# Last row's router scratch moved out of `wout`, longer runs for the final reads, a quarter of the final adds on GpSimd

## The reference, cut to what matters

```python
idx, wts = _router(x, gate_w, e_bias)                 # 6 of 64 experts for each token
shared = _relu2(x @ shared_up_w.T) @ shared_down_w.T
routed = _moe(x, idx, wts, w1, w2)                    # each expert takes at most 64 tokens
return shared + routed

h = _relu2(einsum('ecd,eid->eci', xd, w1))            # in _moe: xd are the tokens in each expert's slots
yd = einsum('eci,edi->ecd', h, w2)
y_assign = yd[e_flat, slot] * gate
zeros((T, D)).at[tok].add(y_assign)
```

## Time and profile before

| | |
|---|---|
| median of 3 runs | 1371.82 us (1371.63 to 1372.96) |
| the profiled execution | 1371.9 us, of which the span from first to last instruction is 1370.1 us |
| busy: PE, DVE, ACT, POOL | 1145.9 us (84%), 912.0 us (67%), 658.6 us (48%), 567.1 us (41%) |
| DMA | 159.56 MB, 116 GB/s over the span |
| chain that ended last | PE 55%, DVE 19%, POOL 7%, issue 7%, ACT 6%, DMA 4% |

### The profile page before, as it was taken

How to read it: one execution, slowest core, us unless ns; L and a number is a source line. 1 busy time by engine, 2 the same in 40 slices (tenths; PEclk the granted TensorE clock), 3 DMA queues, 4 the chain that set the end, 5 groups by cost and what they waited for, 6 DMA issues and landing times.

```text
span 1370.1 us, 24377 instructions
## 1 busy us (share of the span) xinstructions
PE 1145.9 (84%) x8378; PEld 741.5 (54%) x8380; DVE 912.0 (67%) x1850; ACT 658.6 (48%) x1575; POOL 567.1 (41%) x725
## 2 busy tenths in 40 slices
PE   2799998898899888988999988989999978877940
PEld 2355556665555557655555566655555566644520
DVE  4487785565788875656888875656887755671427
ACT  3655423666455524656445335666555235630630
POOL 1255561220377760210577831200777712133760
PEclk9999999999999998998999998999999999989975
DMA  7366442300243314101343332001333625058888
GB/s 312 118 206 196 156 156 74 94 2 20 87 145 108 107 43 118 48 2 35 120 129 101 116 80 70 25 21 39 129 123 106 195 76 162 10 196 268 155 198 313
DMA packets 120137, 159.56 MB, mean 116 GB/s; under 512 B 11632, under 2 KB 82928, under 8 KB 119280
## 3 DMA queue, kind: packets, MB, share of 16 engines
q1 hardware_dynamic: 106384, 131.73, 31.0%
q0 software_dynamic: 9216, 19.98, 5.7%
q10 hardware_dynamic: 4416, 6.29, 1.3%
HBM read 104.55 MB, written 40.83 MB: 106 GB/s over the span
## 4 chain that ended last, share of the span: by engine, by line
PE 55%; DVE 19%; POOL 7%; issue 7%; ACT 6%; DMA 4%; SPq 0%; POOLq 0%; DVEq 0%; ACTq 0%
PE bank L1187 12%; PE bank L1229 5%; DVE pool_c L1689 5%; PE bank L1110 5%; PE bank L1410 3%; PE bank L1367 3%; PE bank L1395 2%; PE bank L1332 2%; PE bank L1223 2%; PE bank L1216 2%; PE bank L1208 2%; PE bank L1300 2%; POOL joint L2198 2%; PE bank L1497 2%; POOL xn L2205 2%
## 5 line engine op out<-in xcount | busy, mean ns | idle before, releaser
L1187 PE MATMUL bank<-xm,joint 128*128 128x512 f32 x544 | 272.8, 626 | 20.2 <-DVE pool_c L1689 15.6
L2198 POOL TENSOR_TENSOR joint<-joint 128x512 f32<-128x512 f32 x128 | 168.5, 1318 | 225.3 <-DVE joint L1705 221.2
L1689 DVE SCALAR_TENSOR_TENSOR pool_c<-bank,params,pool_c 128x511 f32<-128x511 f32 (+2 forms) x216 | 161.1, 747 | 84.8 <-ACT pool_c L812 79.4
L1187 PEld LDWEIGHTS bank<-xm,joint 128*128 128x128 f32 x544 | 99.9, 197 | 123.9 <-issue 93.3
L1889 DVE TENSOR_REDUCE nmax<-bank 128x1 f32<-128x384 f32 (+3 forms) x176 | 109.6, 637 | 60.6 <-PE bank L1368 59.8
L1229 PE MATMUL bank<-wout,pool_c 128*128 128x256 f32 x512 | 125.1, 388 | 3.4 <-DVE pool_c L1730 3.4
L851 ACT ACTIVATE joint<-bank,dt_ 128x64 f32<-128x64 f32 x512 | 112.0, 342 | 28.7 <-PE bank L1110 28.7
L1229 PEld LDWEIGHTS bank<-wout,pool_c 128*128 128x128 f32 x512 | 98.6, 196 | 38.7 <-issue 23.3
L821 ACT ACTIVATE pool_c<-pool_c 128x512 f32<-128x512 f32 x64 | 40.2, 629 | 143.5 <-DVE pool_c L1689 143.5
L2192 POOL DMA_INDIRECT xslot<-xrow,slots x96 | 97.3, 1013 | 26.6 <-issue 21.9
L1730 DVE TENSOR_TENSOR pool_c<-xn,pool_c 128x512 f32<-128x512 f32 x64 | 90.0, 1405 | 19.1 <-POOL xn L2205 19.0
(11 more groups left out here) (272 smaller groups left out, 2379.1 us busy)
## 6 DMA issues: line engine op xcount, KB each, us to landing
pool_b<-dA_rows SPq DMA_DIRECT2D x64, 256.0 KB
pool_b<-dec_rows SPq DMA_DIRECT2D x96, 128.0 KB, 3.6
joint<-pool_b SPq DMA_DIRECT2D x96, 128.0 KB, 2.4
acc<-xrow SPq DMA_DIRECT2D x13, 640.0 KB, 6.1
joint<-dA_rows SPq DMA_DIRECT2D x32, 256.0 KB, 3.2
dA_late<-dA_rows SPq DMA_DIRECT2D x32, 256.0 KB, 4.1
joint<-acc SPq DMA_DIRECT2D x32, 256.0 KB, 6.7
xslot<-xrow SPq DMA_DIRECT2D x16, 321.0 KB, 4.8
```

The source lines that it names most:

```text
L1187: last = mm(bank[:, :], win[:, k, col:col + P], xm[:, k, :], start=(k == 0), stop=(k == KD - 1))
L1689: ins = v.scalar_tensor_tensor(out=cv[:, n:L], in0=bank[:, 0:L - n], scalar=convw[:, ci, TAPS - 1 - n:TAPS - n], in1=cv[:, n:L], op0=ALU.m ...
L2198: M_ready.inc(p.tensor_tensor(M[u % 2][:, hs_, :], Lx[:, hs_, :], cbm[:, c * P:(c + 1) * P].unsqueeze(1).to_broadcast([P, 4, P]), ALU.mult))
```

## The change

1. The scratch of the last row's router goes to a tensor of its own (`last_rt`, 1736 elements for each partition) and to `xm` and the end of `mixed`; the router's scratch is packed closer in all rows. `wout` is then free as soon as the last mixer is done: four pairs of weights go there in group 1 instead of three in group 3 and one in group 2. Group 1 has 9 pairs, group 2 has 15, group 3 and its wait for the slots are gone.
2. In the final sums a partition holds 16 consecutive tokens. Copies 0 and 1 are read with one transfer of 2 MB each (runs of 16 KB). The others are read in five reads (`READS`): three of two blocks (runs of 4 KB), then two of one block. Stores follow the same five steps.
3. Copy 4 += copy 5 moves from VectorE to GpSimd; VectorE's last add of a block waits for it (`pool_sum`).

```diff
-        routers.append(Router(wout_[:, 0:2048], wout_[:, 2048:2816], wout_[:, 2816:3328], pob[:, :, :].rearrange("p t n -> p (t n)")))
+        last_rt = sb("last_rt", [P, 1736])
+        routers.append(Router(last_rt, xm[:, :, :].rearrange("p k n -> p (k n)")[:, 0:768], mixed[:, 1024:1536],
+                              pob[:, :, :].rearrange("p t n -> p (t n)")))
...
-        in_row = places(ffnw, 0, W1 + W2) + places(flat(xnT), 0) + places(flat(xn), 0) + places(mixed, 0)
-        in_scores, in_values = places(pool_a, *range(0, 8192, W1 + W2)), places(pool_c, *range(0, 8192, W1 + W2))
-        in_slots = places(wout_, 0, 1024, 2048)
-        wm = in_win + in_row + in_scores + in_values + in_slots
-        loads_of = [len(in_win), len(in_row), len(in_scores) + len(in_values), len(in_slots)]
+        in_row = places(ffnw, 0, W1 + W2) + places(flat(xnT), 0) + places(flat(xn), 0) + places(mixed, 0) + places(wout_, 0, 1024, 2048, 3072)
+        in_scores, in_values = places(pool_a, *range(0, 8192, W1 + W2)), places(pool_c, *range(0, 7168, W1 + W2))
+        wm = in_win + in_row + in_scores + in_values
+        loads_of = [len(in_win), len(in_row), len(in_scores) + len(in_values)]
...
+        sums = [homes[q // 2][:, q % 2 * BLOCKS * BLOCK_T * D:(q % 2 + 1) * BLOCKS * BLOCK_T * D] for q in range(SUMS)]
+        def columns(lo, hi):
+            return slice(lo * BLOCK_T * D, hi * BLOCK_T * D)
+        part_sum = [[sums[q][:, columns(i, i + 1)] for q in range(SUMS)] for i in range(BLOCKS)]
+        READS = [(0, 2), (2, 4), (4, 6), (6, 7), (7, 8)]
+        read_of = [n for n, (lo, hi) in enumerate(READS) for _ in range(lo, hi)]
...
+        def load_sums(eng, loaded, q, lo, hi):
+            loaded.inc(eng.dma_start(sums[q][:, columns(lo, hi)],
+                                     tokens_of(acc[q * (NTOK + CAP):q * (NTOK + CAP) + NTOK, :])[:, columns(lo, hi)]))
...
             load_weights(2)
-            sp.wait_ge(slots_ready.sem, slots_ready.upto(2, b))
-            load_weights(3)
...
             wait_set(sp, 0)
-            for g in range(BLOCKS):
-                load_sums(sp, g, range(2))
+            for q in range(2):
+                load_sums(sp, first_loaded, q, 0, BLOCKS)
...
-                for q in range(2, SUMS, 2):
-                    pair_sum.inc(v.tensor_tensor(parts_[q], parts_[q], parts_[q + 1], ALU.add))
+                pair_sum.inc(v.tensor_tensor(parts_[2], parts_[2], parts_[3], ALU.add))
                 dve.wait_ge(first_sum.sem, g + 1)
                 dve.wait_ge(pair_sum.sem, pair_sum.last())
                 pair_sum.inc(v.tensor_tensor(parts_[0], parts_[0], parts_[2], ALU.add))
                 dve.wait_ge(pair_sum.sem, pair_sum.last())
+                dve.wait_ge(pool_sum.sem, g + 1)
                 final_sum.inc(v.tensor_tensor(parts_[0], parts_[0], parts_[4], ALU.add))
...
+            for g, parts_ in enumerate(part_sum):
+                pool.wait_ge(sums_loaded[read_of[g]].sem, 16 * (SUMS - 2))
+                pool_sum.inc(p.tensor_tensor(parts_[4], parts_[4], parts_[5], ALU.add))
```

More of the change, by code:

```diff
@@ L120, in __init__ @@
         self.wsum, self.wrec = rt[:, 1152:1156], rt[:, 1156:1160]
-        self.s8, self.masked, self.sel, self.nos = tiles(1160, 32), tiles(1280, 256), tiles(1536, 256), tiles(1792, 32)
+        self.s8, self.masked, self.sel, self.nos = tiles(1160, 32), tiles(1192, 256), tiles(1448, 256), tiles(1704, 32)
         self.eoh = eoh
@@ L314, in build @@
         homes = (joint[:, 0:8192], pool_a, pool_c)
-        part_sum = [[homes[q // 2][:, (2 * i + q % 2) * BLOCK_T * D:(2 * i + q % 2 + 1) * BLOCK_T * D] for q in range(SUMS)]
-                    for i in range(BLOCKS)]
+        sums = [homes[q // 2][:, q % 2 * BLOCKS * BLOCK_T * D:(q % 2 + 1) * BLOCKS * BLOCK_T * D] for q in range(SUMS)]
[4 more added lines that the diff above has]
+        read_of = [n for n, (lo, hi) in enumerate(READS) for _ in range(lo, hi)]
+        assert len(read_of) == BLOCKS
         sum_at = sb("sum_at", [P, SETS])
@@ L371, in build @@
         first_loaded = signal("first_loaded", 16)
-        sums_loaded = [signal(f"sums_loaded{i}", 16) for i in range(BLOCKS)]
+        sums_loaded = [signal(f"sums_loaded{i}", 16) for i in range(len(READS))]
+        pool_sum = signal("pool_sum")
         first_sum, pair_sum, final_sum = signal("first_sum"), signal("pair_sum"), signal("final_sum")
@@ L601, in wait_cleared, with tokens_of @@
             eng.wait_ge(cleared.sem, cleared.upto(2 * UNITS))
[L603 to L606, removed]
+        def tokens_of(rows):
+            return rows.rearrange("(p j) d -> p (j d)", p=P)
+        def load_sums(eng, loaded, q, lo, hi):
+            loaded.inc(eng.dma_start(sums[q][:, columns(lo, hi)],
+                                     tokens_of(acc[q * (NTOK + CAP):q * (NTOK + CAP) + NTOK, :])[:, columns(lo, hi)]))
         row_loads = [(wq, a["wq"]), (wk, a["wk"]), (wv, a["wv"]), (wo, a["wo"]), (su, a["su"]), (sd, a["sd"])]
@@ L746, in _ @@
             wait_set(sp, 0)
-            for g in range(BLOCKS):
-                load_sums(sp, g, range(2))
+            for q in range(2):
+                load_sums(sp, first_loaded, q, 0, BLOCKS)
             for s in range(1, SETS):
                 wait_set(sp, s)
[L751 to L757, removed]
+            for n, (lo, hi) in enumerate(READS):
+                for q in range(2, 4):
+                    load_sums(sp, sums_loaded[n], q, lo, hi)
+            for lo, hi in READS:
+                sp.wait_ge(final_sum.sem, hi)
+                out_stored.inc(sp.dma_start(tokens_of(a["out"].rearrange("b l d -> (b l) d"))[:, columns(lo, hi)], sums[0][:, columns(lo, hi)]))
+            sp.wait_ge(out_stored.sem, 16 * len(READS))
         @block.scalar
@@ L1100, in _ @@
                 wait_set(act, s)
-            for g in range(BLOCKS):
-                load_sums(act, g, range(4, SUMS))
+            for n, (lo, hi) in enumerate(READS):
+                for q in range(4, SUMS):
+                    load_sums(act, sums_loaded[n], q, lo, hi)
         @block.tensor
@@ L2138, in _ @@
                 targets(i)
-            dve.wait_ge(first_loaded.sem, 16 * 2 * BLOCKS)
-            for g in range(BLOCKS):
-                parts_ = part_sum[g]
+            dve.wait_ge(first_loaded.sem, 16 * 2)
+            for parts_ in part_sum:
                 first_sum.inc(v.tensor_tensor(parts_[0], parts_[0], parts_[1], ALU.add))
-            for g in range(BLOCKS):
-                parts_ = part_sum[g]
-                dve.wait_ge(sums_loaded[g].sem, 16 * (SUMS - 2))
-                for q in range(2, SUMS, 2):
-                    pair_sum.inc(v.tensor_tensor(parts_[q], parts_[q], parts_[q + 1], ALU.add))
+            for g, parts_ in enumerate(part_sum):
+                dve.wait_ge(sums_loaded[read_of[g]].sem, 16 * (SUMS - 2))
+                pair_sum.inc(v.tensor_tensor(parts_[2], parts_[2], parts_[3], ALU.add))
                 dve.wait_ge(first_sum.sem, g + 1)
```

## The result

The changed kernel takes 1376.04 us (median of 8 runs, 1374.65 to 1380.34), the kernel before 1372.12 us beside it (8 runs). The ratio is 1.0029, with a 95% interval of 1.0018 to 1.0040: slower by 0.29%, 3.9 us. One execution of e1, a kernel of the table further down, took 1439.03 us at a lower granted clock (0.817) and is not in e1's ratio.

The account below looks back on a forecast made before the run. The end was taken to have two close limits, VectorE's adds and 8.4 MB of reads plus 2.1 MB of stores. 1371.9 less 3.2, less 0.6, plus 1.0, plus 2.6, plus 3.1 gave 1374.8 us; range 1369.0 to 1378.2.

Parts of the forecast that it names:

- Weights earlier: Four pairs' weights moved from behind attention to its middle: last scatter lands sooner, gain 3.2 us, bounds 0.6 and 4.2.
- The landing taken: Last scatter, once the weights are out of its way: 3.5 us to land, near the earlier rows' median of 3.0.
- The rival in which the scatter gains nothing: Weights still fill the engines at 1249 us, scatter lands in 6.1 us, clock falls: 1378.0 us, chance 0.10.
- TensorE's clock: First pairs of the last row: earlier tokens start TensorE before the clock falls, gain 0.6 us, between 0 and 1.7.
- Copies 0 and 1 in two transfers: Reads beside the last accumulating adds: 1.0 us more, bounds 5.5 less and 2.4 more.
- the packet rival: Copies 0 and 1: 16 KB packets keep accumulating adds out, upper bound 2.4 us instead of 1.0; 1376.2 us, chance 0.17.
- The sign it named: Beside the reads of copies 0 and 1: accumulating adds of 9 us and more would show the packets at work.
- Larger first read: Start of the final sums: VectorE waits for two blocks instead of one, 2.6 us more.
- One add in four on GpSimd: Final sums: each of eight GpSimd adds delays VectorE by 1.0 us; run 25.1 us, 3.1 more than before.
- The faster rival: Final sums: GpSimd's adds don't exclude VectorE's, last term minus 1.5 us; 1367.6 us, chance 0.13.
- the whole 1.27 us: Final sums: by the skill page's rule each GpSimd add costs VectorE up to this, bringing the run to 27.3 us.
- The pairs: Last row's expert pairs, up to the reads of copies 0 and 1: the forecast sum had no term of their own.

Follow-up runs that it names:

- e1: Kernel before with part 1 alone (router scratch moved, four pairs' weights loaded during attention): 1369.45 us, ratio 0.9984 to the kernel before.
- e11: Part 1 alone on the kernel before, with 74 instead of 58 products that nobody reads: 1368.04 us, ratio 0.9966 to the kernel before.
- e12: e11 with the final sums of e7, on the kernel before's own reads (eight blocks, 2 KB runs): 1368.15 us, ratio 0.9966 to the kernel before.
- e2: Changed kernel with copy 4 += copy 5 back on VectorE: 1375.16 us, ratio 1.0027 to the kernel before.
- e3: Changed kernel with copies 0 and 1 read in 16 transfers with 2 KB runs: 1377.55 us, ratio 1.0034 to the kernel before.
- e4: Changed kernel with the first final read of two blocks cut into two of one block: 1376.03 us, ratio 1.0034 to the kernel before.
- e7: Changed kernel with copy 3 copied to PSUM by ScalarE, giving each VectorE add one PSUM input: 1372.33 us, ratio 1.0003 to the kernel before.
- e6: Changed kernel with all final reads of one block, eight reads: 1374.96 us, ratio 1.0021 to the kernel before.
- e10: Part 1 alone on the kernel before, with old router scratch offsets kept in rows 0 to 2: 1368.66 us, ratio 0.9967 to the kernel before.
- e8: e7 with the 2 KB first reads of e3 and final reads of one block save one: 1370.94 us, ratio 0.9990 to the kernel before.

## Why the prediction was right, point by point

The forecast was 1374.8 us, and 1376.04 was measured: slower, for the reasons given, with terms that erred on both sides. That the sum came so close is in part luck: against the ledger the terms for copies 0 and 1 and for the clock were 1.5 and 1.2 us too low, and those for the weights, GpSimd and the pairs 0.9, 0.4 and 1.1 too high.

- **Weights earlier:** 3.2 us put, 4.1 measured (G to T). The landing taken, 3.5 us, was too long; the 2.69 measured lie near the other bound, 2.5. The rival in which the scatter gains nothing fell. The weights went at 1155 to 1172 us and not in the idle stretch from 1172 that the prediction named; they show no cost there either.
- **TensorE's clock:** a gain of 0.6 put, none measured (T to D is 0.6 longer). The fall came with the tokens. e11 and e12 show 1.1 to 2.1 us to be had in this stage by keeping TensorE at work until they land; no time shows them.
- **Copies 0 and 1 in two transfers:** 1.0 put, 2.5 measured in the pair of traces, about 2 over all. This is the term that was mis-sized most. The value was taken near rows of 2 KB runs, though the prediction had the upper bound, 2.4, with its mechanism as the packet rival. The sign it named came, an add of more than 9 us (12.02; 12.49 in e2), and e3 takes it away. In this term the rival was right and the forecast was not, and the rival's time, 1376.2 us, is the nearer one. The rule of the Trainium skill, DMA: Bandwidth & Descriptors, section "Queues, rings and completion order", a whole packet of one queue before the next, was the better guide than the rows with short runs. The trace of after agrees with it: 173 packets of the adds beside 176 of the reads, shown at e3.
- **Larger first read:** 2.6 put, 2.55 measured (A to V). e4 adds what the sum didn't say: with single blocks in front only, the next read is late instead.
- **One add in four on GpSimd:** 3.1 put, 2.7 measured. Each of GpSimd's eight adds cost VectorE 0.955 us (7.64 by 8), against 0.9 to 1.07 put and 1.0 taken. e2 and e7 show the mechanism. The faster rival needed adds that stay at 0.69 us; they did not. By the whole 1.27 us for each add the run would have been 27.3 us; it was 24.72.
- **The pairs** (D to F) took 1.1 us less than before, which the sum did not have. The stage ranges from 50.6 to 52.6 us over the fourteen traces, with and without part 1, so nothing is read from it.

The stages of the two traces differ by 3.15 us where 2.9 were put. The medians differ by 3.9, with an interval from 2.5 to 5.5 us (0.18 to 0.40% of 1372). Of the three losses, the times alone show that on VectorE, by e7; e2, e3, e4 and e6 take back a term in their traces, and their intervals overlap that of after. Over the runs the medians of kernels with part 1 come out a little worse than their stages: e1 by 1.4 us, e10 by 1.8, e11 by 1.0, e12 not at all. That would fit a later start of the last row, and its cause is open, as said at e10.

## What to carry to other kernels

Before an add is moved to GpSimd, see where its neighbours on VectorE have their inputs: with both in SBUF, 32 adds on VectorE alone were done 2.8 us sooner than 24 beside GpSimd's eight, while with one input in PSUM the same split saved 6 us of run. With the reads of after that split also beat the kernel without one (27.69 us from A to E in e7, 30.26 in e2); with the reads of before it gained nothing (27.48 in e12, 27.42 in e11), because the copies stood behind the reads. Longer runs gave the final reads a little more rate (418 GB/s with 4 KB against 404 with 2 KB, from 1346 to 1354 us); beside accumulating adds that others wait for they kept an add out for 12 us. And where an earlier transfer is to help TensorE, look at its clock at the moment of landing: the products that kept it at work shortened the next stage in two traces, though no time shows it.

## What the runs showed that was not expected

- A queue that also computes: 14 and 16 issues on ScalarE took 7.64 and 9.56 us, and its own copies stood behind them (e8, e12).
- The granted clock fell between 1253 and 1254 us in after, some 3 us after the products nobody reads had ended (1250.3), and between 1257 and 1258 in e1, where they had ended at 1252.1 and other products had already run again; it was back some 7 us later in both. In e10 it fell between 1258 and 1259 us and was back between 1262 and 1263. In e11 and e12, without the gap, it did not fall.
- The exclusion works on GpSimd too. In e6 its eight adds took from 1.26 to 1.77 us, in e12, with VectorE in PSUM, from 1.25 to 1.27.
- Executions of kernels with the same work in rows 0 to 2 began the last row up to 3.5 us apart (913.08 to 916.59 us).
